# A convolution in the Hartley domain: the load phase with block transposes on VectorE and four-lane tables

## The reference

```python
pooled = x.mean(axis=(2, 3))
lf = tanh(((pooled @ conv_w.T) - bn_mean) * (bn_gamma / sqrt(bn_var + 1e-5)) + bn_beta)   # 8 groups x 9 taps
low = sum over the 9 shifted copies (reflect padding) of x * lf                            # per group of 4 channels
x = (low * (inside_all + 1) - inside_all * gap) * lamb_l + x * (lamb_h + 1)                # gap: channel means

x_ht = dht_2d(x)
out_ht[:, :, :20, :20] = compl_mul2d(x_ht[:, :, :20, :20], w1)                             # mixes 32 -> 32 channels
y = dht_2d(out_ht) / (H * W)
y = gaussian_smoothing_4d(y)          # 9-tap blur over batch, channel, height, width, edge padding
return y * (abs(fftfreq(W)) <= 0.25)  # 65 of 128 columns survive
```

## Time and profile before

| | |
|---|---|
| median of 3 runs | 195.07 us (193.82 to 197.18) |
| the profiled execution's own time | 193.97 us |
| its span, first to last instruction | 192.1 us |
| mean granted TensorE clock | 0.929 of full speed |
| TensorE busy (matmul) | 169.2 us, 88% |
| VectorE busy | 87.1 us, 45% |
| ScalarE busy | 81.3 us, 42% |
| GpSimd busy | 39.4 us, 21% |
| DMA | 36.76 MB, 191 GB/s over the span; 19.76 MB read, 16.78 MB written |

### The profile page before, as it was taken

How to read it: one execution, slowest core, us unless ns; L and a number is a source line. 1 busy time by engine, 2 the same in 40 slices (tenths; PEclk the granted TensorE clock), 3 DMA queues, 4 the chain that set the end, 5 groups by cost and what they waited for, 6 DMA issues and landing times.

```text
span 192.1 us, 4416 instructions
## 1 busy us (share of the span) xinstructions
PE 169.2 (88%) x1778; PEld 109.5 (57%) x1778; DVE 87.1 (45%) x189; ACT 81.3 (42%) x149; POOL 39.4 (21%) x21
## 2 busy tenths in 40 slices
PE   6589999999999999999999988999999999983500
PEld 3135656656564564656685778868767876761200
DVE  0002357198676868757456990223334333431200
ACT  2169774665565564564520091134343333331100
POOL 8992003008052160704204200000000000000000
PEclk9889999999999999999995599999999999999555
DMA  6999999999956366000000000008799999999997
GB/s 182 295 280 304 305 339 303 335 309 293 286 175 211 99 213 195 0 0 0 0 2 0 0 0 3 3 7 246 200 291 282 280 291 283 286 282 289 285 278 225
DMA packets 43795, 36.76 MB, mean 191 GB/s; under 512 B 692, under 2 KB 35676, under 8 KB 43780
## 3 DMA queue, kind: packets, MB, share of 16 engines
q1 hardware_dynamic: 43780, 36.54, 66.0%
HBM read 19.76 MB, written 16.78 MB: 190 GB/s over the span
## 4 chain that ended last, share of the span: by engine, by line
PE 71%; DMA 10%; SPq 4%; ACT 4%; DVE 3%; issue 2%; DVEq 0%
PE ps L381 15%; PE ps L413 12%; PE ps L550 11%; PE ps L391 9%; DMA x_ring<-x 5%; DMA out<-rows 5%; PE ps L509 5%; PE ps L529 4%; PE ps L400 4%; PE ps L401 4%; SPq L345 4%; PE ps L487 3%; ACT mixin L605 2%; PE ps L422 2%; ACT y_sb L617 1%
## 5 line engine op out<-in xcount | busy, mean ns | idle before, releaser
L381 PE MATMUL ps<-x_ring,k_wide 128*64 128x512 f32 x128 | 35.4, 632 | 3.6 <-DMA x_ring<-x 3.6
L550 PE MATMUL ps<-cols,k_wide 128*128 128x396 f32 (+2 forms) x96 | 31.7, 480 | 4.1 <-ACT rows L580 4.1
L617 ACT COPY y_sb<-ps 128x448 f32<-128x448 f32 x32 | 29.7, 933 | 9.9 <-PE ps L391 9.9
L612 ACT COPY freq<-ps 128x512 f32<-128x512 f32 x32 | 18.7, 586 | 29.7 <-PE ps L381 29.1
L391 PEld LDWEIGHTS ps<-k_wide,freq 128*128 128x128 f32 x128 | 13.7, 143 | 25.5 <-issue 24.4
L413 PEld LDWEIGHTS ps<-k_wide,y_sb 128*128 128x128 f32 x192 | 23.5, 194 | 7.3 <-ACT y_sb L617 4.2
L413 PE MATMUL ps<-k_wide,y_sb 128*128 128x44 f32 x192 | 24.8, 283 | 0.6 <-ACT y_sb L617 0.2
L550 PEld LDWEIGHTS ps<-cols,k_wide 128*128 128x128 f32 x96 | 17.8, 193 | 13.3 <-issue 5.3
L580 DVE COPY rows<-ps 128x396 f32<-128x396 f32 (+2 forms) x24 | 12.0, 502 | 22.6 <-PE ps L550 12.9
L580 ACT COPY rows<-ps 128x396 f32<-128x396 f32 (+1 forms) x24 | 11.1, 481 | 25.4 <-DMA out<-rows 13.5
L391 PE MATMUL ps<-k_wide,freq 128*128 128x128 f32 x128 | 21.5, 292 | 0.1
(11 more groups left out here) (66 smaller groups left out, 140.4 us busy)
## 6 DMA issues: line engine op xcount, KB each, us to landing
out<-rows SPq DMA_DIRECT2D x7, 1152.0 KB, 9.6
out<-rows SPq DMA_DIRECT2D x8, 896.0 KB, 8.7
w_sb<-mix_w SPq DMA_DIRECT2D x2, 960.0 KB, 10.1
out<-rows SPq DMA_DIRECT2D x3, 384.0 KB, 3.5
x_ring<-x SPq DMA_DIRECT2D x2, 512.0 KB, 5.3
k_wide<-wide SPq DMA_DIRECT2D x1, 533.0 KB, 7.8
x_ring<-x SPq DMA_DIRECT2D x15, 0.5 KB, 9.2
k_wide<-wide SPq DMA_DIRECT2D x1, 225.0 KB, 2.9
```

Of the source, the lines that this page charges most:

```text
L381: last = nc.tensor.matmul(ps[half * 64:half * 64 + 64, g % 2, :], const(O_LT, (1, 64)), x_ring[:, u, at:at + G1 // 2 * H], start=True, sto ...
L550: nc.tensor.matmul(ps[:, B_F[k % 3], 0:nt * NW], const(O_LH + s * H, (1, H)), cols[:, u, t:t + nt, :], start=True, stop=True).then_inc(f_d ...
L612: nc.scalar.copy(freq[:, g % 2, :], ps[:, g % 2, :]).then_inc(freq_out, 1)
L617: nc.scalar.copy(view(y_sb[:, u, 0, g * G1:g * G1 + 1], (1, G1 // 2), (G1 // 2, 2), (C, NP)), view(ps[:, 2 + g % 2, 0:1], (128, G1 // 2), ...
```

## The change

It replaces the way from image to coefficients, for all eight images, and leaves mixing and the store phase alone.

- *Layout.* 32 row-frequency slots for cosines and 32 for sines, ordered (j, index), index running over six frequencies and two edges. Stage 1 puts columns 0 to 63 of eight channels in PSUM partitions 0 to 63 and columns 64 to 127 in partitions 64 to 127, into four banks, one per group.
- *Transposes.* `turn_group`, `keep_freq` and `keep_y` go. VectorE turns 32 x 32 blocks from PSUM straight into `y_sb`: `turn_y`, two an image, 1024 numbers a partition each; and stage 2's result into `data`: `turn_data`, 512 numbers.
- *Stage 2.* The basis is stationary in tables of 32 columns, `y_sb` moves: 16 products of 256 columns, in four lanes of 32 output partitions (one per j).
- *Logits* as one column: `conv_sb` stationary, the channel sums moving; tanh with bias and scale in one ScalarE instruction, and `kb` (74 x 32, double-buffered) by a second one.
- *Coefficients* in four lanes: for each bank (396 and 504 columns) one product per j, each with its own columns of a table of 80 x 3600 numbers (1.152 MB). The parts have 21 columns in place of 20, from which the mirrored half is read backwards.
- *Sum* over the nine planes: four additions instead of one reduction.
- *Pipeline* unrolled on TensorE, ScalarE and VectorE. The tables' load stands behind the second half of image 1. At the end the order is stage 2, two idle products, logits, two idle products, coefficients, eight idle products.

```diff
 # TensorE
-            def stage1(n, it, u, g):
+            def stage1(n, g):
...
+                if n and g % 2 == 0:
+                    pe.wait_ge(y_ready, (n - 1) * UNITS + g // 2 + 1)
+                for side in range(2):
+                    at = g * G1 * H + side * 64
+                    last = nc.tensor.matmul(ps[side * 64:side * 64 + 64, g, :], const(O_LT, (1, YC)),
+                                            view(x_ring[:, u, at:at + 1], (H, G1), (1, 64)),
+                                            start=True, stop=True)
                 last.then_inc(s1_done, 1)
+            def stage2(n):
+                pe.wait_ge(y_ready, (n + 1) * UNITS)
+                if n:
+                    pe.wait_ge(data_out, n)
+                for part in range(2):
+                    for side in range(2):
+                        for j in range(J):
+                            last = nc.tensor.matmul(
+                                ps[32 * j:32 * j + 32, B_DATA, part * C * IDX:(part + 1) * C * IDX],
+                                const(O_RU + (part * 2 + side) * FN, (1, FN)),
+                                view(y_sb[:, n % 2, 0, side, j * IDX:j * IDX + 1], (YC, C), (1, IDX)),
+                                start=(side == 0), stop=(side == 1))
+                last.then_inc(s2_done, 1)
+            def filter_logits(n):
+                if n == 0:
+                    pe.wait_ge(params_in, 32)
+                else:
+                    pe.wait_ge(tanh_done, n)
+                pe.wait_ge(data_out, n + 1)
+                nc.tensor.matmul(ps[0:GROUPS * TAPS, B_LF, 0:1], conv_sb[:, :], data[0:C, n % 2, 0, 0, 0:1],
+                                 start=True, stop=True).then_inc(lf_done, 1)
+            def coefficients(n):
+                if n == 0:
+                    pe.wait_ge(table_in, 16)
+                else:
+                    pe.wait_ge(coef_used, n)
+                pe.wait_ge(kb_done, n + 1)
+                for bank, lo, size in ((0, 0, ND + NA), (1, ND + NA, NB)):
+                    for j in range(J):
+                        at = j * NTAB + lo
+                        last = nc.tensor.matmul(ps[32 * j:32 * j + 32, B_COEF + bank, 0:size],
+                                                kb[0:KROWS, n % 2, :], table[0:KROWS, at:at + size],
+                                                start=True, stop=True)
+                last.then_inc(coef_done, 1)
...
+            for g in range(NG1):
+                stage1(0, g)
+            for n in range(1, N):
+                stage1(n, 0)
+                stage1(n, 1)
+                stage2(n - 1)
+                stage1(n, 2)
+                filter_logits(n - 1)
+                stage1(n, 3)
+                coefficients(n - 1)
+            stage2(N - 1)
             keep_busy(2)
...
             filter_logits(N - 1)
+            keep_busy(2)
             coefficients(N - 1)
             keep_busy(8)
 # ScalarE
+            def taps(n):
+                act.wait_ge(lf_done, n + 1)
...
+                nc.scalar.activation(tap_tanh[0:GROUPS * TAPS, n % 2:n % 2 + 1], ps[0:GROUPS * TAPS, B_LF, 0:1],
+                                     ACT.Tanh, bias=bn[0:GROUPS * TAPS, 4:5], scale=bn[0:GROUPS * TAPS, 3:4]
+                                     ).then_inc(tanh_done, 1)
+                act.wait_ge(tanh_done, n + 1)
+                if n >= 2:
+                    act.wait_ge(coef_done, n - 1)
+                nc.scalar.activation(kb[0:KROWS, n % 2, :], tap_gain[0:KROWS, :], ACT.Copy,
+                                     scale=tap_tanh[0:KROWS, n % 2:n % 2 + 1]).then_inc(kb_done, 1)
 # VectorE
+            def turn_y(n, unit):
+                dve.wait_ge(s1_done, n * NG1 + 2 * unit + 2)
+                if n >= 2 and unit == 0:
+                    dve.wait_ge(s2_done, n - 1)
+                half = C // 2
+                nc.vector.transpose(
+                    view(y_sb[:, n % 2, unit * half, 0, 0:1], (1, half * YC)),
+                    view(ps[:, 2 * unit, 0:1], (1, half * YC))).then_inc(y_ready, 1)
+            def turn_data(n):
+                dve.wait_ge(s2_done, n + 1)
+                if n >= 2:
+                    dve.wait_ge(lf_done, n - 1)
+                nc.vector.transpose(
+                    view(data[:, n % 2, 0, 0, 0:1], (FN, 2), (2 * FN, IDX), (1, FN)),
+                    view(ps[:, B_DATA, 0:1], (C * IDX, 2), (1, IDX), (IDX, C))).then_inc(data_out, 1)
...
+            def combine_sum(m):
+                base = m * F_LINKS
+                flat = lambda plane, count: view(terms[:, plane, 0:1], (1, count * WIDE))
+                dve.wait_ge(coef_used, m + 1)
+                dve.wait_ge(f_step, base + 3)
-                tr(xht[:, :], view(terms[:, 0, 0:1], (1, PLANE), (PLANE, NTERM)), AX.X, ALU.add).then_inc(f_step, 1)
+                tt(flat(0, 4), flat(0, 4), flat(4, 4), ALU.add).then_inc(f_step, 1)
...                                      # then 2, 1 and 1 planes, each waiting for the one before
+                low = view(terms[:, 0, 0:1], (NB1, Q), (1, MODES))
+                high = view(terms[:, 0, Q * NB1 + MODES:Q * NB1 + MODES + 1], (NB1, Q), (-1, MODES))
+                for part, op in ((0, ALU.subtract), (1, ALU.add)):
+                    last = tt(view(parts[:, m % 2, part, 0:1], (MODES, Q), (1, MODES)), low, high, op)
+                last.then_inc(parts_done, 1)
+            turn_y(0, 0)
+            turn_y(0, 1)
+            prepare()
+            for n in range(1, N):
+                if n >= 2:
+                    combine_products(n - 2)
+                turn_y(n, 0)
+                if n == 2:
+                    dve.wait_ge(rest_in, 16)
+                if n >= 2:
+                    combine_edges(n - 2)
+                turn_data(n - 1)
+                if n >= 2:
+                    combine_sum(n - 2)
+                turn_y(n, 1)
+            combine_products(N - 2)
+            turn_data(N - 1)
+            combine_edges(N - 2)
+            combine_sum(N - 2)
+            combine_products(N - 1)
+            combine_edges(N - 1)
+            combine_sum(N - 1)
 # SyncE
-            sp.dma_start(k_narrow[:, :], narrow).then_inc(narrow_in, 16)
             load(1, 1, 1)
+            sp.dma_start(table[:, :], taps_table).then_inc(table_in, 16)
```

More of the change, by code:

```diff
@@ L59 @@
 NC128 = O_TURN + S * Q * C
[L61 to L70, removed]
+P_A, P_B = 0, C
+P_ONE = 2 * C
+P_GAMMA, P_BETA, P_MEAN, P_VAR = (P_ONE + 1 + i for i in range(4))
+NPAR = P_VAR + 1
 def frequency(s, j, q):
@@ L103, in constants @@
     e2[H - 2], e2[0] = 1, -1
[L104 to L110, removed]
-                a = frequency(s, j, q)
[L112 to L128, removed]
+    lt = np.zeros((H, 2, J, IDX))
+    basis = np.zeros((3, S, Q, NB1))
+    for j in range(J):
+        for s in range(S):
+            for q in range(Q):
+                a = frequency(s, j, q)
+                lt[:, 0, j, s * Q + q] = np.cos(th * a * h)
+                lt[:, 1, j, s * Q + q] = np.sin(th * a * h)
+        lt[:, 0, j, SQ], lt[:, 0, j, SQ + 1] = e1, e2
+    ru = np.zeros((2, 2, FN, H))
+    for b in range(NB1):
+        bb = b % MODES
+        c, sn = np.cos(th * bb * h), np.sin(th * bb * h)
+        ru[0, 0, b], ru[0, 1, b] = c, -sn
+        ru[1, 0, b], ru[1, 1, b] = sn, c
+        basis[:, :, :, b] = np.array([1, np.cos(th * bb), np.sin(th * bb)])[:, None, None]
+    ru[0, 0, NB1], ru[0, 0, NB1 + 1] = e1, e2
+    ru[0, 1, NB1 + 2], ru[0, 1, NB1 + 3] = e1, e2
+    ru = ru.reshape(2, 2, FN, 2, 2, FN).transpose(3, 1, 5, 0, 4, 2)
+    d = np.zeros((KT, J, 2, S, Q, NB1))
+    e = np.zeros((KT, J, 4, S, Q, NB1))
     f = np.zeros((KT, J, 3, S, Q, 8))
@@ L134, in constants @@
                 ea = np.exp(1j * th * a)
-                for b in range(MODES):
-                    bb = column(s, b)
+                for b in range(NB1):
+                    bb = b % MODES
                     eb = np.exp(1j * th * bb)
@@ L188, in constants, with hartley_conv_kernel @@
             wide[q * C:(q + 1) * C, at:at + C] = blur_matrix(C).T
[L190 to L200, removed]
+    table = np.zeros((KPAD, J * NTAB), np.float32)
+    table[:KROWS] = taps.reshape(KT, -1)[[*range(TAPS)] * GROUPS + [TAPS, TAPS // 2]]
+    return wide, table
+def hartley_conv_kernel(nc, x, wide, taps_table, params, conv_wt, mix_w, out):
     fp32 = mybir.dt.float32
@@ L665, in _ @@
+            act.wait_ge(setup, 2)
+            nc.scalar.activation(bn[:, 1:2], bn[:, 0:1], ACT.Sqrt).then_inc(root_done, 1)
+            for n in range(N):
+                taps(n)
             act.wait_ge(last_share, 1)
@@ L810, in combine_sum @@
-                tt(parts[:, u, 1, :], xht[:, 0:half], xht[:, half:], ALU.add).then_inc(parts_done, 1)
-            def load_step(m, u):
-                combine_products(m, u)
-                combine_sum(m, u)
-                taps(m + 1)
-            dve.wait_ge(rest_in, 16)
-            taps(0)
-            for m in range(2):
-                load_step(m, m)
```

(6 more changed lines are left out.)

349 lines of the change are left out of this document (95 added, 254 removed).

## The result

The changed kernel took 175.65 us in the median of four runs, against 195.82 for the kernel before beside it (the profiled executions: 174.56 and 193.97). The ratio is 0.898, 95% interval 0.885 to 0.912: about 10% faster. One of the four executions took 231.71 us, with TensorE's clock at 0.58 of full on average (what rival (d) calls a clock that stayed low); it was not traced, and the ratio leaves it out.

The account below looks back on a forecast made before the run. TensorE bounds the load phase; in the new kernel DMA does until image 4: 46.4 + 4 x 8.1 = 78.8, then the tail to T = 90.9; 193.97 - 18.7 = 175.3 us. Low end 173.3 (faster DMA another 0.7), high end 186.

Parts of the forecast that it names:

- rival (d): TensorE's clock falls at image 4 or mixing, costing 2 to 5 us; staying low, 15 an image; large clock loss 0.05.
- the point T: End of VectorE's last `parts`, of image 7: 90.9 us forecast for 109.6 before, everything behind it unchanged.
- Image 4 at 46.4: Load phase: DMA brings image 4 at 46.4 us, 13.26 MB moved by 45 us plus 1.4 us landing.
- 8.1 us an image: TensorE's time per image in the load phase from image 4 on, for 11.43 before.
- the loss per round: TensorE's products in lanes: each round loses 0.045 us beyond its columns, between ends of 0.02 and 0.07.
- Rival (e): TensorE's changes of tile shape, six an image, cost 0.15 us each: 8.45 an image, 177 us; chance 0.10.
- The placing step: Step after mixing, 32 products in four lanes: 1.40 us for 1.08 of columns, read as 0.02 lost a round.
- VectorE under TensorE: Load phase: VectorE's 7.7 us an image, transposes 3.1 of it, stays hidden under TensorE's 8.1, by 0.4 only.
- (a): VectorE becomes the bound if transposes cost 1.15 times the price or more: 180 at 1.5, 187 at 2; chance 0.13.
- (b): VectorE's transposes from 2.3 times the price: no gain; at 3, 208 us, slower; chance 0.06 together with clock low.
- rival (c): Four lanes run two by two: stage 2 4.0, 11.5 an image, 194 us (0.04 with (f), stores set the end); partly, 180 (0.08).
- GpSimd's hold: Tail: the second step of image 7's edges meets GpSimd's last pass and waits to 88.1 us.

Follow-up runs that it names:

- b_one_free: Kernel before with one transpose per group in place of four, and GpSimd's share of images 1 to 6 cut to one of eight planes: 184.22, 185.26, 207.16, 247.74 us.
- b_one_turn: Kernel before with one transpose of 128 columns per group in place of four, plus four idle products at its start: 215 to 242 us.
- a_late: Changed kernel with both parts of the mixing weights loaded behind image 7 instead of behind images 2 and 3: 172.12 us, ratio 0.892 to the kernel before.
- the pad: Changed kernel with one idle product of 256 columns behind the coefficients of each of images 0 to 6: 176.93 us.
- a_turn_more: Changed kernel with each second VectorE turn of an image, from image 1 on, done twice, the extra one into a scratch tile: 178.3 us.
- a_no_share: Changed kernel without GpSimd's last share, that of image 6: 174.13 us.
- a_split: Changed kernel with GpSimd's last share cut into three pieces of 240 numbers, each multiplied and then added: 176.05 us.
- a_reduce: Changed kernel with one strided reduction of nine planes in place of the four additions: 176.24 us.

## Why the prediction was right

**What bounds it, and the point T:** right. Before, the pace was TensorE's; b_one_free gave back 1.3 us an image for 12 transposes. That is 0.33 a group (four took 0.59, the one left takes 0.26), not the 0.44 of b_one_turn's expectation (0.147 each): here too a part of the 0.59 comes once per group.

**Image 4 at 46.4:** it started at 48.07, 1.7 late. The term that was mis-sized is the rate and the landing: 261 and 311 GB/s for 269 and 315 brings 13.0 MB by 45 us, and the 13.24 MB are through at 45.8; landing took 2.2 us more, not 1.4. a_late shows that it was DMA's queue that set this start: with 1.97 MB moved out of its way, image 4 started 2.36 us sooner.

**8.1 us an image:** it is 7.62. Stage 2 took 1.86 for 2.1, the coefficients 1.65 for 1.7, two stage-1 groups in a row 1.87 for 2.02, and the 0.1 of gaps was not there; the logits took 0.22 for 0.15. The reads of stage 1 in runs of 64 numbers (of eight channels, not images as the prediction has it), bounded by 0 and 0.1, cost nothing: a group alone still takes 1.01. The step that failed is the loss per round. Two groups of stage 1 take 1.87 and one 1.01: a group is then 0.86, its columns (0.865), and 0.15 comes once. Two idle products take 1.06 and one 0.63, so 0.43 and once 0.20. Stage 2 is 1.73 of columns and 0.13 over, the coefficients 1.52 and 0.13. There too it comes once: the records of one lane in stage 2 start 0.240 us apart the first time and 0.216 each time after it, the price of their columns alone. So rounds lose nothing, and each change of shape costs 0.13 to 0.20 us: six at 0.15 and 6.7 us of columns give 7.6. Rival (e) had the right mechanism and a wrong sum: it set them on top of a stage 1 whose 4.04 held four of them already. The Trainium skill's rule (TensorEngine Tiling, Key Properties: changing the tiling mode drains TensorE) agrees with this trace, in which a change costs those 0.13 to 0.20. That it is the change of shape is argued, since no run changes the shape alone. For it speak the pad, which waits for no semaphore and still pays, and stage 2, in which every instruction loads its own stationary and the seven starts after the first show no loss. The placing step, from which the forecast had its 0.02 a round, was read wrongly too: its first rounds of 96 columns start 0.083 us apart, for 0.081 of columns. Where the rest of its 0.32 lies is not worked out.

**The two errors cancel:** 46.4 + 4 x 8.1 = 78.8 was forecast for the end of `coefficients(6)`, and 48.07 + 4 x 7.62 = 78.55 came. The tail, forecast at 12.1, took 12.0. The total is better than its terms, and that is luck.

**VectorE under TensorE:** right. The turns took 1.25 and 0.71 us for 1.21 and 0.68; the Trainium skill's one element per cycle and lane (Vector Engine (DVE) Microarchitecture Reference, 3.8) agrees, 1024 numbers being 1.07 us at its page's 0.96 GHz beside the fixed part. Rivals (a) and (b) fell with that number, though a_turn_more shows that (a) was near: at 0.7 us more it binds.

**Lanes:** rival (c) fell for the order of the change: the four lanes run side by side. With a lane's products in a row, two run at a time, as (c) has it, though in stage 2 alone: 4.53 us for (c)'s 4.0, and 191 us in all.

**GpSimd's hold:** right in place and size, 1.36 us, and nothing in the steady stretch of the kernel after.

**Clock:** TensorE waited 3.2, 1.3 and 0.1 us ahead of images 2, 3 and 4 (3, then 1.5 to 2 and 1.5 to 2 in the forecast). The falls came at 28.3 and 38.6 us, 3.4 us long each, and lengthened stage 1 of images 2 and 3 from 1.9 to 3.4 and 3.6 us. They were absorbed, as forecast, though without anything to spare: `coefficients(2)` ended at 47.9, image 4 landed at 48.0. A fall at image 4, in the traces of a_no_share and a_split, cost some 1.6 us, below the 2 to 5 of (d). The fall at the mixing did not come.

## What to carry to other kernels

When the pace is TensorE's, write its period as columns plus changes of shape, and look in the trace for the same piece once alone and once doubled: the difference separates the two. With narrow outputs in lanes, let the lane index run innermost. And when a phase becomes faster, ask from where on it is the bound: here DMA's order decided the first 48 us, and moving loads that nobody needed yet brought T forward by another 3.6 us.

## What was not expected of the hardware

- TensorE's clock can stay at half (1.2 GHz) under unbroken work: 89 us in b_one_turn, with products of 44, 128, 512 and 480 columns. In the kernel after, the two falls of the load phase ended within 3.4 us, while stage 1 and stage 2 ran.
- A lane's products in a row cost the other lanes half of their overlap: 4.53 us for 1.86. The next lane started beside the lane's fifth pass of eight, ahead of three that still waited.
- GpSimd and VectorE hold each other: where GpSimd's instructions of 240 numbers met VectorE's additions they took 0.88 and 1.02 us for 0.69 and 0.59. Which of the two begins first matters: in a_reduce VectorE's edge step began 0.1 us ahead of GpSimd's addition and took 0.56 us for 1.91, and GpSimd's took 2.02 for 1.70. VectorE's reduction, with one operand, was not held beside it (2.27 us).
